# Two layers of a graph network on 128 graphs: products with W and W2 ahead of the aggregations, on operands transposed by DMA

## What is computed

```python
# layer 0
h = maximum(layernorm(x), 0)
A_hat = A + eye;  d = A_hat.sum(-1) ** -0.5
x = x + (A_hat * d[:, None] * d[None, :]) @ (h @ W + b)          # W is 512 x 512
# layer 1: two hypergraph convolutions, H = (adj != 0), w = first row of adj
h = maximum(layernorm(x), 0)
conv(v, Wt, bias) = Dn * (H @ (Be * (H.T @ (v @ Wt.T)))) + bias  # Dn = 1/(H @ w), Be = 1/column sums of H
z = relu(conv(h, W1, b1));  z = layernorm(z) * gamma + beta      # W1: 512 -> 1024
x = x + (conv(z, W2, b2) + h)                                    # W2: 1024 -> 512
```

## Time and profile before

| | |
|---|---|
| median of 3 executions | 2085.38 us (2084.23 to 2088.61) |
| the profiled execution: its time | 2088.66 us |
| its span, first to last instruction | 2086.9 us |
| PE busy | 2057.0 us, 99% |
| DVE busy | 1809.2 us, 87% |
| POOL busy | 1347.2 us, 65% |
| ACT busy | 1138.8 us, 55% |
| DMA queue | 81.82 MB, 11.9% of 16 engines |

### The profile page before, as it was taken

The page is one execution under the profiler, slowest core; times in us unless marked ns, Lnnn a source line. Parts: engine busy times, 40 slices in busy tenths (PEclk is TensorE's granted clock), DMA queues, the critical chain, the costliest instruction groups (busy, mean ns, idle before and its releaser), DMA issues.

```text
span 2086.9 us, 52719 instructions
## 1 busy us (share of the span) xinstructions
PE 2057.0 (99%) x14614; PEld 1142.3 (55%) x14614; DVE 1809.2 (87%) x4642; ACT 1138.8 (55%) x2097; POOL 1347.2 (65%) x2190
## 2 busy tenths in 40 slices
PE   6999999999999999999999999999999999999998
PEld 3555555555555555555555555555555555555554
DVE  7988888888888888888888888888888888888885
ACT  7555555555555555555555555555555555555543
POOL 4666666666666666666666666666666666666643
PEclk9999999999999999999999999999999999999999
DMA  4011111111111111111111110110111111111100
GB/s 161 30 34 40 39 34 34 40 39 34 36 43 34 34 40 39 34 35 39 39 34 37 42 34 34 40 39 34 35 39 39 34 40 39 34 34 40 39 22 26
DMA packets 58343, 82.10 MB, mean 39 GB/s; under 512 B 6736, under 2 KB 23120, under 8 KB 58320
## 3 DMA queue, kind: packets, MB, share of 16 engines
q1 hardware_dynamic: 58320, 81.82, 11.9%
HBM read 48.24 MB, written 33.55 MB: 39 GB/s over the span
## 4 chain that ended last, share of the span: by engine, by line
PE 97%; issue 1%; POOL 0%; DVE 0%; DMA 0%; SPq 0%; ACT 0%; POOLq 0%; DVEq 0%; ACTq 0%
PE ps_c L370 48%; PE ps_y L370 32%; PE ps_c L359 3%; PE ps_t L359 3%; PE ps_t L361 3%; PE ps_t L360 3%; PE ps_c L360 3%; PE ps_c L361 3%; PE ps_a L453 1%; DMA adj_first<-in_adj_dram 0%; PE ps_p L479 0%; PE ps_p L480 0%; SPq L301 0%; PE ps_y L388 0%; PE ps_d L410 0%
## 5 line engine op out<-in xcount | busy, mean ns | idle before, releaser
L753 DVE SCALAR_TENSOR_TENSOR z<-ps_c,dn,b_all 128x512 f32<-128x512 f32 x256 | 189.9, 742 | 156.1 <-PE ps_c L370 156.1
L631 ACT ACTIVATE hn_hi<-h,nm,sc 128x1024 f16<-128x1024 f32 x128 | 158.8, 1241 | 233.8 <-POOL nm L1251 233.8
L1202 POOL TENSOR_TENSOR scr<-x1b,xh 128x512 f32<-128x512 f32 x128 | 278.6, 2177 | 0.7 <-ACT xh L597 0.5
L1143 POOL TENSOR_TENSOR rd<-u,neg_half 128x2 f32<-128x2 f32 x128 | 136.3, 1065 | 202.4 <-DVE u L827 202.4
L558 ACT ACTIVATE h<-z 128x512 f32<-128x512 f32 x256 | 161.0, 629 | 193.9 <-DVE z L753 186.2
L1238 POOL TENSOR_SCALAR u<-st 128x1 f32<-128x1 f32 x128 | 90.6, 708 | 271.2 <-DVE st L952 271.1
L370 PE MATMUL ps_c<-w1h,t1h 128*128 128x512 f16 x1024 | 262.4, 378 | 2.5 <-DVE t1l L932 2.5
L370 PE MATMUL ps_c<-w1l,t1h 128*128 128x512 f16 x1024 | 263.0, 379 | 0.1
L370 PE MATMUL ps_c<-w1h,t1l 128*128 128x512 f16 x1024 | 262.8, 379 | 0.0
L612 ACT ACTIVATE P_hi<-ps_p 128x128 f16<-128x128 f32 x128 | 35.4, 277 | 414.3 <-PE ps_t L361 414.1
L370 PE MATMUL ps_y<-w2h,t2h 128*128 128x512 f16 x1024 | 243.5, 381 | 3.0 <-issue 3.0
(11 more groups left out here) (140 smaller groups left out, 5410.2 us busy)
## 6 DMA issues: line engine op xcount, KB each, us to landing
out_dram<-out_t SPq DMA_DIRECT2D x128, 256.0 KB, 2.0
x_t<-in_x_dram SPq DMA_DIRECT2D x126, 256.0 KB, 2.6
adj_t<-in_adj_dram SPq DMA_DIRECT2D x126, 64.0 KB, 1.8
raw_w<-in_W1T_dram SPq DMA_DIRECT2D x4, 512.0 KB, 6.5
raw_w<-in_W2T_dram SPq DMA_DIRECT2D x8, 256.0 KB, 8.2
raw_w<-in_W_dram SPq DMA_DIRECT2D x4, 256.0 KB, 4.5
b_all<-in_b_dram SPq DMA_DIRECT2D x2, 256.0 KB, 7.8
x_first<-in_x_dram SPq DMA_DIRECT2D x2, 256.0 KB, 7.7
```

The source lines that it names most:

```text
L631: act.activation(hn_hi[:, :], h[:, :], ACT.Identity, bias=nm2[:, m:m + 1], scale=sc2[:, m:m + 1])\
L753: dve.scalar_tensor_tensor(out=z[:, cols], in0=Y1[n][:, :], scalar=dn1[:, m:m + 1], in1=b1_all[:, cols], op0=ALU.mult, op1=ALU.add).then_i ...
L1202: pool.tensor_tensor(scr2[:, g % 2, :], x1b[:, :], xh[:, :], ALU.add).then_inc(s_scr2, 1)
```

## The change

The aggregation and the product with the weights change places in two of the three products. Layer 0 computes h0 @ W first (Y0), adds the bias (`yv`, y in SBUF), splits it (yh, yl) and multiplies by A (Z0, three matmuls of 512 columns in `spread`). The second convolution of layer 1 computes hn @ W2 first (U), splits it (uh, ul) and multiplies by P (Y2, again `spread`). For this the stationary operands must be h0 and hn transposed: SP issues four DMA transposes per graph from SBUF to SBUF, of h0_hi and h0_lo (128x512 float16, 128 KB each) and hn_hi and hn_lo (128x1024, 256 KB each). The first convolution (T1, Y1a, Y1b) stays. ROW, T0, T2, DEG, s_in, base0, d_hi and d_lo go; the two columns for the degrees ride in the moving operand of P (130 columns). adj, x, A and P have four buffers instead of two, the loop takes four graphs per turn, and all orders are new.

```diff
-    LOOP_TO = NG - 4
-    assert (LOOP_TO - LOOP_FROM) % 2 == 0 and LOOP_TO > LOOP_FROM
+    LOOP_TO = NG - 6
+    assert (LOOP_TO - LOOP_FROM) % 4 == 0 and LOOP_TO > LOOP_FROM
...
+        T1, Y0, AY = ps_c0, ps_e, ps_e
...
+            with nc.Fori(0, LOOP_TO - LOOP_FROM, 4, engines=(eng_type,), hint_back_edge=True) as i:
+                count = {c: engine.to_reg(i + c) for c in range(LOOP_FROM - 5, LOOP_FROM + 10)}
...
+            def transposed(dst, g, src, loaded):
+
+                width = src.shape[1]
+                slot = dst[:, g % 2 * width:(g % 2 + 1) * width].rearrange("p (c r) -> p c r", r=128)
+                sp.dma_start_transpose(slot, src[:, :]).then_inc(loaded[g % 2], 16)
+
+            def do_trh(g, i=0):
+                settled(sp)
+                sp.wait_ge(s_hnh, upto(i, g))
+                wait(sp, s_u, i, g - 2)
+                transposed(hnT_hi, g, hn_hi, s_trh)
...
+            def step(i, k):
+                do_tr0h(k + 1, i)
+                do_trh(k - 2, i)
+                do_trl(k - 2, i)
+                do_tr0l(k + 1, i)
+                do_st(k - 4, i)
+                do_ldX(k + 4, i)
+                do_ldA(k + 4, i)
...
+            def spread(ps, lhs_hi, lhs_lo, rhs_hi, rhs_lo):
+
+                pe.matmul(ps, lhs_hi, rhs_hi, start=True, stop=False)
+                pe.matmul(ps, lhs_hi, rhs_lo, start=False, stop=False)
+                return pe.matmul(ps, lhs_lo, rhs_hi, start=False, stop=True)
...
+                pe.matmul(ps_p[:, 0:N + 2], H_T[:, m, :], HB_w[:, m, :], start=True, stop=False)
+                pe.matmul(PP, H_T[:, m, :], HB_lo[:, :], start=False, stop=True).then_inc(s_p, 1)
+
+            def do_U(g, i=0):
+                cols = slice(g % 2 * DH, (g % 2 + 1) * DH)
+                wait_transposed(pe, s_trh, i, g)
+                wait(pe, s_uh, i, g - 1)
+                wait(pe, s_ul, i, g - 1)
...
+                spread(ps_y2[:, :], P_hi[:, r, :], P_lo[:, r, :], uh[:, :], ul[:, :]).then_inc(s_y2, 1)
+
+            def do_Y0(g, i=0):
+                cols = slice(g % 2 * DIN, (g % 2 + 1) * DIN)
+                wait_transposed(pe, s_tr0h, i, g)
+                wait(pe, s_x1, i, g - 1)
...
+                spread(AY[:, :], A_hi[:, r, :], A_lo[:, r, :], yh[:, :], yl[:, :]).then_inc(s_ay, 1)
...
+                act.activation(uh[:, :], ps_u[:, :], ACT.Copy, scale=U_EVAC).then_inc(s_uh, 1)
...
+                act.activation(yh[:, :], y[:, :], ACT.Copy, scale=Y_EVAC).then_inc(s_yh, 1)
...
+                dve.scalar_tensor_tensor(out=x1[:, m, :], in0=AY[:, :], scalar=cx[:, m:m + 1], in1=x_of(g),
...
+                dve.scalar_tensor_tensor(out=ul[:, :], in0=ps_u[:, :], scalar=U_EVAC, in1=uh[:, :],
...
+                dve.scalar_tensor_tensor(out=y[:, :], in0=b_sc[:, :], scalar=rd0[:, m, 1:2], in1=Y0[:, :],
...
+                dve.scalar_tensor_tensor(out=yl[:, :], in0=y[:, :], scalar=Y_EVAC, in1=yh[:, :],
```

More of the change, by code:

```diff
@@ L117, in bass_adjacency_prenorm_two_layer_gnn_kernel @@
         h0_hi, h0_lo = sb("h0_hi", [128, DIN], F16), sb("h0_lo", [128, DIN], F16)
[L118 to L120 removed]
+        h0T_hi, h0T_lo = sb("h0T_hi", [128, 2 * DIN], F16), sb("h0T_lo", [128, 2 * DIN], F16)
+        y = sb("y", [128, DIN])
+        yh, yl = sb("yh", [128, DIN], F16), sb("yl", [128, DIN], F16)
         x1 = sb("x1", [128, 2, DIN])
@@ L141, in bank @@
             return ctx.enter_context(nc.psum_tensor(name, [128, n * CH], F32))
-        ps_t2 = bank("ps_t2", 2)
+        ps_e = bank("ps_e")
+        ps_u = bank("ps_u")
         ps_c0 = bank("ps_c0")
@@ L236, in wait_dma, with adj_of, x_of, wait_transposed @@
                 eng.wait_ge(pair[g % 2], i * 8 + 16 * (g // 2 + 1))
[L238 to L250, removed]
-        def wait_load(eng, sems, i, g):
[L253 to L262, removed]
+        def adj_of(g):
+            return adj_t[:, g % 4, :]
+        def x_of(g):
+            return x_t[:, g % 4, :]
+        def wait_load(eng, sems, i, g):
+            eng.wait_ge(sems[g % 4], i * 4 + 16 * (g // 4 + 1))
+        def wait_transposed(eng, pair, i, g):
+            if not isinstance(i, int) or g >= 0:
+                eng.wait_ge(pair[g % 2], i * 8 + 16 * (g // 2 + 1))
+        def steady(engine, eng_type, step):
+            nonlocal count
+            with nc.Fori(0, LOOP_TO - LOOP_FROM, 4, engines=(eng_type,), hint_back_edge=True) as i:
+                count = {c: engine.to_reg(i + c) for c in range(LOOP_FROM - 5, LOOP_FROM + 10)}
+                for k in range(LOOP_FROM, LOOP_FROM + 4):
+                    step(i, k)
         block = ctx.enter_context(nc.Block())
@@ L343, in _ @@
-            assert LOOP_FROM == 6
-            with nc.Fori(0, LOOP_TO - LOOP_FROM - 4, 2, engines=(ENG.SP,), hint_back_edge=True) as i:
-                step(i, LOOP_FROM)
-                step(i, LOOP_FROM + 1)
-            for k in range(LOOP_TO - 4, NG + 3):
-                step(0, k)
+            do_tr0h(1); do_ldA(5); do_tr0l(1); do_ldX(4); do_tr0h(2); do_ldA(6); do_tr0l(2); do_trh(0)
+            do_trl(0); do_tr0l(3); do_ldX(5); do_tr0h(3); do_ldA(7); do_ldX(6); do_trh(1); do_trl(1); do_st(0)
```

914 lines of the change are left out of this document (451 added, 463 removed).

## The result

The changed kernel takes 1990.4 us (median of 4 runs, 1989.2 to 1991.1) against 2085.5 us before: a ratio of 0.954, 95% interval 0.953 to 0.956. The prediction was 1986 us, 1974 to 2060, faster with 0.84. The profiled execution took 1990.5 us, its span 1988.7; the one of before took 2088.7.

The account below looks back on a forecast made before the run. PE, busy 99%, was taken to bound the kernel. From 2088.7 us profiled, 120 steps gaining 0.81 us (97) and 3 at start and end gave 1988.7; less 3.3 for the median, 1985.4, said as 1986, range 1974 to 2060.

Parts of the forecast that it names:

- PE sets the pace through its own work: In the steady part PE is busy 99% and its matmul prices explain the 15.93 us step with no gap.
- -0.81 us per step: Net change of PE's work per graph in the steady part, bringing the step to 15.13 us.
- DVE does not become the bound: DVE's work per step falls from 14.0 to 13.3 us, 88% of the new 15.13 us step.
- slack at Z0: Z0 needs yl, made from Y0; PE has 3.45 us between, DVE needs 2.7, leaving about 0.6 us after draining.
- 0.4 to 1.6: Slack in us at T1, which needs xh_lo; DVE has 7.8 us after Z0 for its list.
- small waits: Rival: PE waits a little each step, at Z0 or T1, 0.1 to 0.6 us, giving 2000 to 2058 us; chance 0.20.
- hn_hi is ready 2.5 us into the step, hn_lo 5.45: When ACT and DVE finish the two parts of hn, so that their transposes for U can start.
- They may take 7.4 us: Transposes of hn, 256 KB each, may take 7.4 and 8.0 us from issue to landing before PE waits at U.
- L + 7.8: Step in us if the loop U, uh, t1h, hn_hi, transpose of time L sets it; slow-transposes rival, chance 0.13.
- A transpose lands in 2 to 4 us: Time for a 256 KB transpose of hn, taken from plain transfers of that size landing in 2.0 to 2.6 us.
- 27% DMA share: DMA engines' share of a step: 768 KB of transposes at the plain rate, 2.3 us, on top of 1.75.
- Start and end -3, +-10: Outside the steady part, 3 us of gain, half of at most 6.5, with 10 us either way.

Follow-up runs that it names:

- pe_fill14: Changed kernel with 14 extra matmuls of 128 columns per graph behind U, into a PSUM bank nobody reads: 2083.3 us, ratio 0.998 to the kernel before.
- before_less14: Kernel before the change with 14 low-part matmuls of 128 columns per graph left out: 1993.5 us, ratio 0.955.
- dve_plus2: Changed kernel with two extra DVE operations of yl's kind and size right ahead of yl: 2209.8 us, ratio 1.059.
- lat2: Changed kernel with two tiny DMAs, each waited for, ahead of each transpose of hn_hi: 2008.9 us, ratio 0.963.
- lat3: Changed kernel with three tiny DMAs, each waited for, ahead of each transpose of hn_hi: 2102.6 us, ratio 1.008.
- tr_double: Changed kernel with a second transpose of the same size, of constant data into a spare buffer, behind each of the four: 2008.0 us, ratio 0.962.
- copies: Changed kernel with plain on-chip DMA copies of the same bytes in place of the four transposes: 1985.3 us, ratio 0.951.
- layer0_back: Changed kernel with layer 0 in its old form, without its bias row: T0 in Y0's place, products with W in Z0's: 2092.4 us, ratio 1.003.

## Why the prediction came true, step by step

*PE sets the pace through its own work.* Right, and shown from both sides (pe_fill14, before_less14).

*-0.81 us per step.* Measured -0.79. The pitches of 0.216 and 0.056 held in Z0, Y2 and U.

*DVE does not become the bound.* Right by the sum: 13.3 us a step were predicted, by the 0.88 that the earlier trace rows give, 175.76 / 200 x 15.13 = 13.3 measured. The slack at Z0 was put at 0.6; yl ends at 1010.87 and Z0 starts at 1011.65, so 0.78. At T1, xh_lo ends at 1003.45 and T1 starts at 1004.93: 1.48, inside the 0.4 to 1.6. Small waits did not come: DVE's operations of 0.68 start 0.60 apart, which makes up for the hand-overs. But the prediction missed a term: DVE's durations were taken as fixed. Two of the experiments show one growing by 1.07 us when it meets POOL's addition that has already begun. In the changed kernel yl starts 0.62 us ahead of that addition. Had the new order put it a little over 0.62 us later, it would have ended 0.62 + 1.07 = 1.69 us later, 0.9 beyond the slack, and the rival "small waits" would have come true with some 110 us. That is worked out from dve_plus2, not run. The prediction saw the small slack, but not what decides whether it holds: that yl stood ahead of the addition was luck, as far as the prediction goes.

*hn_hi is ready 2.5 us into the step, hn_lo 5.45.* Their transposes were issued at 2.66 and 5.41.

*They may take 7.4 us.* lat2 (6.2 us, step unchanged) and lat3 (7.97, step 15.77) bracket it, and L + 7.8 gave the step to 0.01 us. The parts that the prediction lists (0.6, 0.6, 1.24 and 5.18) add up to 7.62; the other 0.2 it did not name, and 7.79 was measured.

*A transpose lands in 2 to 4 us.* Measured 3.1 and 3.2, and 2.4 for those of h0. *27% DMA share:* wrong, 39%. The step that failed is the one that priced a transpose at the plain rate: 768 KB took about (0.39 - 0.12) x 15.13 = 4.1 us of all engines and not 2.3. It cost nothing, because the transposes are hidden: tr_double has a share of 0.65 and PE does not wait in the middle. That pieces smaller than rows cost more holds for the same bytes, not for a piece: the transposes' packets are mostly under 512 B, and they took 1.8 times the DMA time of the copies, but the whole queue had 3.5 times as many packets as in copies (467,920 against 132,048) in 1.5 times the time (40.1% against 27.0% of 16 engines). SP's issue took 1.23 us for one of hn and 1.2 for one of h0 with half the bytes. At the same size a transpose landed later than a copy, 3.1 against 2.3 us.

*Start and end -3, +-10.* Measured 98.1 - 95 = 3. The size is right, its reason only in part: copies shows that transposes cost 4 to 5 us there, so the rest of the change brought more than I gave it.

*What the numbers missed.* 1985.4, said as 1986, against 1990.4. Of these 5.0 us, 1.8 lie in the profiled execution (1988.7 against 1990.5: 120 x 0.02 us of step are 2.4, the rest makes up 0.6), and 3.2 in how it stands to the median: 3.3 us were taken off for that, and the profiled one of the changed kernel stands only 0.1 above its median.

## What to carry to other kernels

Where one engine is busy all of the time, price its instructions by the distances between starts, make the new step's clock from them, and then give every other engine and queue a date on that clock; the sum gives the gain, and the dates say whether it is kept. Moving a product to the other side of an aggregation changes both: layer 0 gave 0.08 us by columns, but in the changed kernel the long product behind T1 covers operations of ACT and DVE, and with a short one in its place (layer0_back) the step was 0.69 us longer. A transfer that took 6.2 us cost the step nothing, and at 7.97 us it set the step, so work out the loop it lies in and what its other members take. And when PE's work changes places, everything that it waits for must move ahead too: with one ACT operation left in its old place a variant was 31% slower than before.
